# A decoder layer on one core: the experts' x of groups 2 and 3 turned by transfers instead of TensorE

## The reference, cut to what matters

```
x = layernorm(x + attention(x))
x = layernorm(x + experts(x, weights=ctx_512, ensembles=itok))   # 8 experts, 256 -> 512 -> 256, relu between
x = layernorm(x + ffn(x))                                        # ternary weights, 256 -> 1024 -> 1024 -> 1024 -> 256

h    = relu(einsum('edi,bsi->bsed', proj_in, x))
o    = einsum('eid,bsed->bsei', proj_out, h)
gate = einsum('bks,bkse->bse', weights, one_hot(ensembles))
return einsum('bsei,bse->bsi', o, gate)
```

## Time and profile before

| | us |
|---|---|
| median of 3 runs (759.05 to 759.16) | 759.11 |
| the profiled execution, its own time | 760.14 |
| its span, first to last instruction | 758.2 |
| TensorE busy | 746.4 |
| VectorE busy | 597.3 |
| ScalarE busy | 431.3 |
| GpSimd busy | 244.6 |

### The profile page before, as it was taken

One profiled execution on the slowest core, in us unless ns is written; L12 is line 12 of the kernel. 1 busy time (PEld: TensorE's weight loads), 2 busy tenths in 40 slices (PEclk: granted clock), 3 DMA queues, 4 the chain that ended last, 5 costly groups with the idle time before them and its releaser, 6 DMA issues.

```text
span 758.2 us, 11840 instructions
## 1 busy us (share of the span) xinstructions
PE 746.4 (98%) x3699; PEld 630.9 (83%) x3699; DVE 597.3 (79%) x1308; ACT 431.3 (57%) x843; POOL 244.6 (32%) x278
## 2 busy tenths in 40 slices
PE   8999999999999999999999999999999999999996
PEld 6788888888888888888888888888778988888886
DVE  4789979876698999989866667976976749769566
ACT  5788743344465655546443338456756655566773
POOL 2776243233574755747443231000000200100003
PEclk9999999999999999999999999999999999999998
DMA  7800000002445526362452111044435100373201
GB/s 248 322 2 0 2 1 1 1 1 90 175 153 174 164 81 208 97 208 97 146 214 57 28 61 31 1 167 143 163 128 177 57 1 20 147 222 115 108 1 59
DMA packets 31706, 77.15 MB, mean 102 GB/s; under 512 B 8736, under 2 KB 13472, under 8 KB 27808
## 3 DMA queue, kind: packets, MB, share of 16 engines
q1 hardware_dynamic: 31360, 76.18, 29.8%
q10 hardware_dynamic: 288, 0.26, 0.1%
HBM read 58.08 MB, written 16.78 MB: 99 GB/s over the span
## 4 chain that ended last, share of the span: by engine, by line
PE 88%; DVE 4%; ACT 3%; issue 2%; DMA 1%; POOL 1%; SPq 0%; DVEq 0%; ACTq 0%
PE bank L1378 16%; PE bank L1234 11%; PE bank L1528 10%; PE bank L1529 10%; PE bank L1262 8%; PE bank L1356 8%; PE bank L1361 8%; PE bank L1357 8%; PE bank L1377 6%; PE bank L1381 2%; DVE part_r L2027 1%; ACT hring L1146 1%; PE bank L1535 1%; PE bank L1536 1%; DMA wp_lo_f<-in_wproj 1%
## 5 line engine op out<-in xcount | busy, mean ns | idle before, releaser
L1378 PE MATMUL bank<-wx_both,hx_hi 128*128 128x512 f32 x512 | 191.4, 397 | 0.0
L1528 PE MATMUL bank<-hring,wring 128*128 128x512 f32 x448 | 174.5, 390 | 2.4 <-DVE part_r L2027 1.3
L989 ACT ACTIVATE hx_hi<-bank 128x512 fp32r<-128x512 f32 x128 | 76.4, 597 | 175.3 <-PE bank L1361 174.2
L1529 PE MATMUL bank<-part_r,wring 128*128 128x512 f32 x448 | 174.3, 389 | 0.0
L720 POOL TENSOR_TENSOR x_tok<-right,x_tok 128x256 f32<-128x256 f32 x128 | 94.6, 740 | 172.0 <-ACT right L996 168.7
L2027 DVE TENSOR_TENSOR part_r<-part_f,hring 128x512 fp32r<-128x512 f32 x144 | 95.3, 689 | 48.7 <-ACT hring L1146 48.5
L1800 DVE SCALAR_TENSOR_TENSOR hx_lo<-bank,hx_hi 128x512 fp32r<-128x512 f32 x128 | 87.9, 687 | 51.4 <-ACT hx_hi L989 49.9
L1378 PEld LDWEIGHTS bank<-wx_both,hx_hi 128*128 128x128 f32 x512 | 96.0, 188 | 16.7
L1377 PE MATMUL bank<-wx_both,hx_lo 128*128 128x256 f32 x384 | 108.6, 283 | 0.0
L1528 PEld LDWEIGHTS bank<-hring,wring 128*128 128x128 f32 x448 | 84.1, 188 | 20.7 <-DVE part_r L2027 1.7
L1529 PEld LDWEIGHTS bank<-part_r,wring 128*128 128x128 f32 x448 | 84.1, 188 | 17.4
(11 more groups left out here) (209 smaller groups left out, 1418.0 us busy)
## 6 DMA issues: line engine op xcount, KB each, us to landing
wring<-h_dram SPq DMA_DIRECT2D x28, 1024.0 KB, 4.8
wx_raw<-in_wx SPq DMA_DIRECT2D x16, 512.0 KB, 7.6
raw_quads<-in_wffn SPq DMA_DIRECT2D x16, 512.0 KB, 5.6
h_dram<-sums SPq DMA_DIRECT2D x8, 1024.0 KB, 4.4
h_dram<-raw_quads SPq DMA_DIRECT2D x8, 512.0 KB, 6.6
stage<-in_wffn SPq DMA_DIRECT2D x12, 256.0 KB, 2.7
x_tok<-in_x SPq DMA_DIRECT2D x1, 2048.0 KB, 10.9
h_dram<-raw_quads SPq DMA_DIRECT2D x8, 256.0 KB, 6.8
```

The source lines that it names most:

```text
L1378: mm = pe.matmul(DBANK[j][:, :].rearrange("p (h d) -> p h d", h=2), hx_hi[:, place, c, a], wo_hl[:, :, c], start=(c == 0), stop=(c == XC - 1))
L1528: pe.matmul(into[:, :], w, b_hi[:, k], start=(k == 0 and i in (0, 1, 3)), stop=False, skip_group_check=True)
L1529: mm = pe.matmul(into[:, :], w, b_lo[:, k], start=False, stop=(k == KH - 1), skip_group_check=True)
```

## The change

Groups 2 and 3 are no longer turned by TensorE: turned stands only in front of the last slot of n = 0 (group 1). Instead ScalarE's split_rows(g + 2) writes the normed rows of a group as 16-bit halves, four copies of 128x512, at c == 2 of the second half of steps 0 and 1. SP issues four transposing transfers. ScalarE's joined_words(g + 1) joins the halves to words at c == 1 of the next step's first half, four copies again, and high_words takes the place of halves_x at c == 2; VectorE's low_words the place of its halves_x at c == 3. For these groups both read x_words in SBUF and not PSUM.

So that the rows are normed in time, VectorE's rows_added(g + 2, c) goes from the second half of step g to its first half, and the norm of group g + 2 to c == 1 of the second half (that of group 1 stays at c == 0 of step 0). GpSimd's root(g + 2) goes in front of all four rows of the second half. VectorE's loop over steps 0 and 1 is written out.

```diff
@@ SyncE, ahead of load_expert(0, 2, 7)
+            for g in range(2, G):
+                for j in range(J):
+                    sp_.wait_ge(s_x_halves, (g - 2) * J + j + 1)
+                    sp_.dma_start_transpose(x_sides[:, j].rearrange("p h c s -> p (h c) s"), x_halves[:, j].rearrange("p h d -> p (h d)")
+                                            ).then_inc(s_x_sides, 16)
             load_expert(0, 2, 7)
@@ GpSimd
+                if further:
+                    root(g + 2)
                 for j in range(J):
-                    if further and j == 2:
-                        root(g + 2)
                     right_added(g * 2 + 1, g, j)
@@ ScalarE
+            def split_rows(g):
+                for j in range(J):
+                    act.wait_ge(s_xn_ok, g * J + j + 1)
+                    act.activation(x_halves[:, j], x_tok[:, g * J + j].bitcast(U16).rearrange("p (d h) -> p h d", h=2), ACT.Copy).then_inc(s_x_halves, 1)
+
+            def joined_words(g):
+                act.wait_ge(s_x_sides, (g - 1) * J * 16)
+                for j in range(J):
+                    act.activation(x_words[:, :, j * S:j * S + S].bitcast(U16).rearrange("p c (s h) -> p c s h", h=2),
+                                   x_sides[:, j].rearrange("p h c s -> p c s h"), ACT.Copy).then_inc(s_x_words, 1)
+
+            def high_words(g):
+                for j in range(J):
+                    act.wait_ge(s_x_words, (g - 2) * J + j + 1)
+                    act.activation(xT_hi[:, :, bass.ds((g * J + j) * S, S)], x_words[:, :, j * S:j * S + S], ACT.Copy).then_inc(s_xThi_ok, 1)
...
+                    if c == 1 and front and g > 0:
+                        joined_words(g + 1)
                     if c == 2 and front:
-                        halves_x(g + 1)
+                        halves_x(g + 1) if g == 0 else high_words(g + 1)
...
+                    if c == 2 and g < G - 2:
+                        split_rows(g + 2)
@@ TensorE
-                    if n % 2 == 0 and n < 2 * G - 2 and c == 3:
+                    if n == 0 and c == 3:
                         turned(n // 2 + 1)
@@ VectorE
                 def step(g, front, further):
                     for c in range(XC):
                         if c == 3 and front:
-                            halves_x(g + 1)
+                            halves_x(g + 1) if g == 0 else low_words(g + 1)
                         low(g * 2 + 1, 1, c, c % 2)
-                        if c == 0 and front:
-                            norm_apply(lambda j: group_row(g + 1, j), lambda j: group_row(g + 1, j), g + 1, s_rstd_ok, s_xn_ok)
+                        if c == 0 and g == 0:
+                            rows_normed(1)
+                        if further:
+                            rows_added(g + 2, c)
                         gated(g * 2, g, c, 0)
...
                     for c in range(XC):
                         low(g * 2 + 2, 0, c, c % 2)
-                        if further:
-                            rows_added(g + 2, c)
+                        if further and c == 1:
+                            rows_normed(g + 2)
                         gated(g * 2 + 1, g, c, 1)
...
-                with dve.Fori(0, G - 2) as g:
+                for g in range(G - 2):
                     step(g, True, True)
```

More of the change, by code:

```diff
@@ L145, in decoder_kernel @@
         sums = at("sums", o_w + 16384, [2, 4, PIECE])
+        x_halves, x_sides = at("x_halves", o_w + 16384, [J, 2, D], U16), at("x_sides", o_w + 20480, [J, 2, DC, S], U16)
+        x_words = at("x_words", o_w + 24576, [DC, N])
         rounded = at_r("rounded", o_w + 57344, [2, PIECE])
@@ L249, in decoder_kernel @@
         s_xT_mm = sem("xT_mm")
+        s_x_halves = sem("x_halves")
+        s_x_sides = sem("x_sides")
+        s_x_words = sem("x_words")
         s_xThi_ok = sem("xThi_ok")
@@ L1796, in halves_x, with low_words @@
                                           xT_hi[:, :, cols].bitcast(F32), ALU.subtract).then_inc(s_xTlo_ok, 1)
+                def low_words(g):
+                    for j in range(J):
+                        dve.wait_ge(s_xThi_ok, g * J + j + 1)
+                        cols = bass.ds((g * J + j) * S, S)
+                        dve.tensor_tensor(xT_lo[:, :, cols], x_words[:, :, j * S:j * S + S], xT_hi[:, :, cols].bitcast(F32), ALU.subtract).then_inc(s_xTlo_ok, 1)
                 def low(unit, place, c, b):
@@ L1815, in rows_added, with rows_normed @@
                         norm_means(g * J, s_bn_ok, s_mv_ok, s_ve_ok)
+                def rows_normed(g):
+                    norm_apply(lambda j: group_row(g, j), lambda j: group_row(g, j), g, s_rstd_ok, s_xn_ok)
                 def step(g, front, further):
```

## The result

The changed kernel takes 762.59 us, median of 7 executions (761.89 to 766.35), the kernel before 759.16 in the same set: ratio 1.0052, 95% interval 1.0043 to 1.0061. It is slower by 0.5%. The forecast was 760.4 with a range of 758.9 to 761.8: the side that the sum gave is right, the size is not, and the range does not hold it.

The account below looks back on a forecast made before the run. TensorE, busy 746.4 of 758.2 us, was taken to bound the kernel. The profiled 760.14 - 1.81 + 2.8 + 0.3 gave 761.43; on the timed runs' median, 759.11 + 1.29 = 760.4 us, range 758.9 to 761.8.

Parts of the forecast that it names:

- part 3: Group 2's new chain of split, transfers and join: VectorE's low_words late in step 1, +0.3 us, bounds 0 and 1.3.
- so nothing later gives a shift back: Expert weights, roots and transfers behind TensorE are released by its own counts, so every shift counts in full.
- the pitch of the slots: Experts' part: plain slots of one up and one down stand 2.76 us apart, taken over for the changed kernel.
- Part 1, the transposes: TensorE's slots with transposes of groups 2 and 3 become plain, saving 0.92 and 0.89 us, together -1.81.
- Part 2, the sums in front: Step 0: three sums before group 1's low halves make TensorE wait for VectorE, +2.8 us, bounds 2.6 to 3.5.
- ScalarE's xT_hi: Near 116 us TensorE's up starts some 0.85 us late for ScalarE's high halves of group 1, within the 2.8.
- no margin: Group 2's transfers all land at T + 5.0, ScalarE comes to joined_words at T + 5.3: just in time.
- rival C: Split, transfer and join take longer than 7.1 us, so low_words slips: 761.6 us; chance 0.14, including a granted-clock fall.
- low_words takes 1.4: VectorE's low halves of group 2 in step 1 take 1.4 us, ending at T + 12.2 against TensorE's T + 12.0.
- mild collision: VectorE's sum beside GpSimd's addition took 0.82 us for 0.48, ending at 119.51, not 119.70 as "fully blocks" would give.
- chance of 0.38 for slower: Chance of a slower kernel: rival C's 0.14 plus 0.24 for the upper third of the forecast's own case.
- within 0.2%: A time of 757.6 to 760.6 us, about what a measurement can tell from no change; chance 0.51.

Follow-up runs that it names:

- -1.81 alone: The kernel before with TensorE's transposes of groups 2 and 3 left out, and with them that part of the computation: 758.79 us, ratio 0.9989.
- increments: The changed kernel with 32 semaphore increments put at TensorE's start, nothing else changed: 765.96 us, ratio 1.0073 to the kernel before.
- sums behind: The changed kernel with step 0's four sums all at c = 3, after the low halves of group 1 (L1825): 761.42 us, ratio 1.0038.
- late gates: The changed kernel with gates of experts 2 and 3 for groups 0 and 1 in steps 2 and 3, step 0's sums at c = 0, 1, 3: 759.47 us.
- sums spread out: The kernel with late gates, but group 2's sums at c = 1, twice at c = 3, the last in the next half: 758.53 us, ratio 0.9988.
- part 2 alone: The kernel before with the change's order of sums, norm and root, loop written out, TensorE still turning the rows: 763.12 us, ratio 1.0045.

## Why the prediction was wrong

Three steps of the prediction failed. The term of part 3, +0.3, was mis-sized: it measured 1.16. The step "so nothing later gives a shift back" put the part behind the experts at nothing: 0.5 was lost there. And the pitch of the slots was taken over as fixed, where it can be longer by 3.6 us in all. The range was too narrow even for its own sum: the upper bounds given, 3.5 and 1.3, come to 762.1, above its end of 761.8.

**Part 1, the transposes: right.** -1.81 foreseen, -1.80 measured, -1.81 alone. "So nothing later gives a shift back" was wrong by 0.5 to 0.8 us, by way of the code fetch.

**Part 2, the sums in front: right, to 0.1 us.** L1825 was to end at 119.57 and ended at 118.87, with the experts 0.57 earlier; TensorE paid 2.69 + 0.11 for 2.8. That the sum comes out to the tenth is in part luck: the wait was 1.64 and not 1.9, and the small losses around it made up for it. The collisions were as weighed: the sums at 112.94 and 115.49 took 0.53 and 0.55 for 0.47. What the text made of the way was half wrong: the first 0.66 is not a wait for ScalarE's xT_hi but for the bank of an up that VectorE's late low halves (L1836) held, 0.40 on the timeline. Either way it is a part of the 2.8. The 0.82 of the earlier trace rows holds no address work of the loop, as the prediction has it elsewhere: it is the meeting with GpSimd alone, since the written-out sums take 0.82 as well.

**Part 3, the chain of group 2: the term was mis-sized,** 0.3 foreseen, 1.03 + 0.13 measured, inside the bounds of 0 to 1.3. The transfers are as priced: SP issues the four in 5.25 us, the last has landed at 133.51, and joined_words began at 134.37, so there was a margin of 0.9 and not "no margin", and rival C is not it. On ScalarE's timeline of the kernel after:
```profile
126.34 2.18 ACT L998 ACTIVATE x_halves<-x_tok 128x512 uint16<-128x512 uint16 x4
...
134.37 2.44 ACT L1003 ACTIVATE x_words<-x_sides 128x512 uint16<-128x512 uint16 x4
136.70 0.59 ACT L1015 ACTIVATE hx_hi<-bank 128x512 fp32r<-128x512 f32 x1
```
The split is the 2.1 foreseen, the join 0.3 longer, which puts a relu to 136.70 and lets VectorE stand for 0.25. The three sums of this half took 0.82, 0.75 and 0.82, each beside an addition of GpSimd, where I had allowed the range from no collision to full. And low_words took 1.97 for 1.4, for the SBUF operand that the copy from the bank had not had: the step "low_words takes 1.4" carried over a row of another form. These 0.57 us are the largest part of the 0.86 by which the term was too small; 0.2 came before low_words, and the rest is what TensorE loses around a wait, for which the sum had no term. The Trainium skill (SBUF — State Buffer, Who interferes with whom) says that of VectorE and GpSimd the loser of their port "fully blocks". If the whole instruction had to wait, the second subtraction of L1832, begun at 140.51 during an addition that ended at 141.19, would have ended near 141.61 (141.19 and its own 0.42); it ended at 141.47. The sums end 0.28 after the addition too, where their own 0.47 would be expected. So the measurement fits a block of all but the first 0.14 to 0.19 us of the instruction (an estimate from 0.42 and 0.47 less 0.28). It is not the mild collision that the prediction read from the earlier trace rows: that sum simply began 0.20 into the addition.

**Not in the sum at all: the pitch and the granted clock,** +3.6 us in some executions and, where the clock fell, +1.6. I took the slot's 2.76 as fixed, and no row priced a fall. The pitch's share is shown for profiled executions: 766.35, 765.86 and 767.44 of the changed kernel with and without increments had 2.800 x107; 760.92 (sums behind) and 759.46 (late gates) had 2.767 for the same 107 slots. That the other executions divide in the same way is argued from their times and mean granted clocks of 0.997 or more: three of ten at 764.6 to 765.3 against 760.6 to 761.9 with the sums behind, two of twelve at 763.1 and 763.8 against 758.8 to 760.3 with the late gates. The kernels without a wait in the experts' part, or with transposes after it, spread by 2.1 us at most.

So for an execution without either the account is -0.57 - 1.80 + 2.80 + 1.16 + 0.5 + 0.5 = +2.6 on the profiled execution's 760.14, 762.7, just above the faster four of seven. The median, 762.59, is the slowest of these four; their own is 762.34, so the three disturbed executions moved it by 0.25. Of the 2.2 us by which it missed, 0.86 is the term of part 3 and 0.5 the code fetch; 0.25 is that shift, and the remaining 0.6 is not assigned (the last stretch's 0.5 and the start's -0.57 differ from one execution to the next). The chance of 0.38 for slower was too low: 0.51 stood for "within 0.2%" because 760.4 lay just below its edge of 760.6, with every unknown on the side above.

**Open:** what decides, after a disturbed slot, between 2.767, 2.780 and 2.800; what the two unprofiled executions at 0.994 and 0.995 looked like; and what decides whether the granted clock falls behind a wait of 1.6 us. Also not tried: moving the code fetch by less costly means than increments, which by the rows above should give some 0.6 us to the kernel with the sums spread out.

## What to carry to other kernels

Before work is moved to the front on an engine that looks 79% busy, list what it does in that half step up to the operand that the bound engine asks for; the 0.3 us of slack stood in two rows, and spreading the same sums over the half steps, with eight rows' gates moved to light steps, turned a loss of 0.5% into a gain of 0.1%. Price a moved read by a row of the same sources: an operand that came from a bank and now comes from SBUF can meet GpSimd, and in these traces the instruction then ended 0.28 us after GpSimd's. Where TensorE is the bound, compare the pitch of equal slots before and after, and look when its code is fetched: both can be changed by an edit that was not made for them. And look at several executions' times and granted clocks before explaining one profile: here the profiled one was the slowest of seven.

## What was unexpected of the hardware

- The same fourteen matmuls per slot, with no wait and at a granted clock of 1.00, ran at 2.767 or at 2.800 us for 107 slots in a row, 3.6 us in all, and once at 2.780 for six. It changed at slots with a wait or with transposes; eight added transposes of 0.9 us saved 3.4 us behind them.
- The same wait of 1.6 us was followed by a granted clock of 1.00 in the changed kernel's profiles and of 0.50 for 3.4 us in that with part 2 alone (1.6 us dearer); behind the waits of 0.8 us it stayed, behind that of 3.4 us it fell.
- A sum or subtraction of VectorE with two operands in SBUF that began during an addition of GpSimd ended 0.28 us after that addition, in 78 of 79 cases.
- With a code fetch beside it, a transposing transfer took 4.6 us to its landing instead of 2.5; by this the feed-forward part became 0.3 to 0.8 us longer in seven of fourteen profiles.
- 32 semaphore increments at TensorE's start delayed its first matmul by 4.0 us.
- ScalarE's strided copies of 128x512 16-bit halves took 618 ns to split and 689 to join, about as long as 32-bit ones (0.60 to 0.64 us in the earlier trace rows); SP issued a transposing transfer of that size in 1.27 us, and it landed after 2.5.
